# A two-layer block on one core: exponentials divided by their sums inside the rounds, on GpSimd, and the heads' projection as a product of high and low parts

## What is computed

```python
xn = _layernorm(x, axis=-1)
att = jnp.einsum('bhcq,bhCq->bhcC', q, k) / d_query
att = jnp.where(causal, att, -jnp.inf)
p = jax.nn.softmax(att, axis=-1)
y = jnp.einsum('bhcC,bhCv->bhcv', p, v)
z = jnp.einsum('dvh,bhcv->bcd', W, y) * (math.sqrt(d_embed / d_value) / num_heads)
```

## Time and profile before

| | us |
|---|---|
| median of 3 runs | 1225.01 (1225.0 to 1225.53) |
| the profiled execution, its own time | 1223.34 |
| its span | 1221.5 |
| PE busy | 1194.4 (98%) |
| DVE busy | 987.6 (81%) |
| ACT busy | 821.7 (67%) |
| GpSimd busy | 409.0 (33%) |

### The profile page before, as it was taken

One profiled execution on the slowest core, in us unless ns is written; L12 is line 12 of the kernel. 1 busy time (PEld: TensorE's weight loads), 2 busy tenths in 40 slices (PEclk: granted clock), 3 DMA queues, 4 the chain that ended last, 5 costly groups with the idle time before them and its releaser, 6 DMA issues.

```text
span 1221.5 us, 23916 instructions
## 1 busy us (share of the span) xinstructions
PE 1194.4 (98%) x8892; PEld 887.0 (73%) x8892; DVE 987.6 (81%) x1916; ACT 821.7 (67%) x2174; POOL 409.0 (33%) x362
## 2 busy tenths in 40 slices
PE   8999999999999999999999999999999999999997
PEld 6777777767776777677767776777677767767765
DVE  5878588878896889688968896889688878888786
ACT  6775577567755775577567756775577668767775
POOL 2216420640064007300630073007300759326910
PEclk9999999999999999999999999999999999999999
DMA  7014300410041003100410041004100500000000
GB/s 255 1 28 129 101 1 15 137 61 2 20 131 61 1 29 134 50 1 30 134 49 1 30 139 44 2 30 145 38 2 29 159 24 2 10 11 18 1 10 27
DMA packets 44276, 63.93 MB, mean 52 GB/s; under 512 B 8128, under 2 KB 18368, under 8 KB 43904
## 3 DMA queue, kind: packets, MB, share of 16 engines
q1 hardware_dynamic: 44160, 62.39, 16.1%
HBM read 59.48 MB, written 2.88 MB: 51 GB/s over the span
## 4 chain that ended last, share of the span: by engine, by line
PE 85%; DVE 6%; ACT 4%; POOL 2%; issue 1%; DMA 1%; SPq 1%; POOLq 0%; DVEq 0%
PE psum L1445 14%; PE psum L1401 14%; PE psum L1467 12%; PE psum L64 11%; PE psum L66 10%; PE psum L65 10%; PE psum L1504 5%; PE psum L1410 2%; ACT probs L737 2%; PE psum L1353 1%; DVE mneg L1103 1%; PE psum L1471 1%; DVE stats L1212 1%; PE psum L1680 1%; ACT pt L758 1%
## 5 line engine op out<-in xcount | busy, mean ns | idle before, releaser
L737 ACT ACTIVATE probs<-psum,mneg 128x512 f32<-128x512 f32 (+3 forms) x640 | 329.8, 529 | 131.1 <-DVE mneg L1103 126.8
L1103 DVE TENSOR_REDUCE mneg<-psum 128x2 f32<-128x1024 f32 (+2 forms) x320 | 254.4, 821 | 118.4 <-PE psum L1410 118.2
L1445 PE MATMUL psum<-ident,probs 128*128 128x128 f32 x1600 | 224.8, 278 | 9.0 <-ACT pt L758 3.9
L1094 DVE COPY pt<-psum 128x512 f32<-128x512 f32 x320 | 206.1, 683 | 31.4 <-PE psum L1445 29.2
L1445 PEld LDWEIGHTS psum<-ident,probs 128*128 128x128 f32 x1600 | 176.3, 140 | 42.8 <-issue 24.4
L544 POOL TENSOR_TENSOR qk_lo<-sg,qk_hi 128x512 fp32r<-128x512 f32 x64 | 93.3, 1463 | 164.4 <-ACT qk_hi L781 164.4
L508 POOL TENSOR_TENSOR rstd<-var,mhalf 128x4 f32<-128x4 f32 x7 | 7.1, 1011 | 406.0 <-DVE var L990 406.0
L1467 PE MATMUL psum<-pt,v_all 128*64 128x384 f32 (+5 forms) x1088 | 142.6, 412 | 0.0
L737 ACT ACTIVATION_READ_ACCUMULATOR probs<-psum,mneg 128x1 f32 x640 | 132.2, 207 | 0.0
L1401 PE MATMUL psum<-qk_hi 64*128 64x512 f32 (+7 forms) x640 | 121.5, 375 | 1.3 <-ACT probs L737 1.1
L1467 PEld LDWEIGHTS psum<-pt,v_all 128*64 128x64 f32 (+1 forms) x1088 | 69.5, 135 | 66.2 <-issue 50.7
(11 more groups left out here) (261 smaller groups left out, 2415.6 us busy)
## 6 DMA issues: line engine op xcount, KB each, us to landing
crow<-weights SPq DMA_DIRECT2D x256, 128.0 KB, 3.0
rrow<-sums SPq DMA_DIRECT2D x128, 128.0 KB, 3.0
gu_raw<-in_gu SPq DMA_DIRECT2D x1, 2176.0 KB, 12.7
x_all<-in_x SPq DMA_DIRECT2D x8, 256.0 KB, 5.5
out_rows<-x_all SPq DMA_DIRECT2D x8, 256.0 KB, 2.3
down_raw<-in_down SPq DMA_DIRECT2D x1, 1088.0 KB, 14.5
wqkv_raw<-in_wqkv SPq DMA_DIRECT2D x1, 896.0 KB, 8.0
wqkv_raw<-in_wqkv SPq DMA_DIRECT2D x1, 512.0 KB, 6.3
```

What stands on the lines that cost most here:

```text
L737: last = act.activation(probs[:, h * HALF + PROB[t]:h * HALF + PROB[t] + w], bank[score_bank(rnd, c) + h][:, o:o + w], ACT.Exp, bias=mneg[ ...
L1094: dve.tensor_copy(turned_rows(rnd)[:, s % 2, :, 3 - s // 2, :], bank[TURN_BANK[s]].rearrange("p (j q) -> p j q", q=P)).then_inc(pt_ready, 1)
L1103: last = dve.tensor_reduce(mneg_h[:, :, t], psum[:, b:b + 2, o:o + P * (t + 1)], AX, ALU.max, negate=True)
L1445: last = nc.tensor.transpose(bank[TURN_BANK[s]][:, i * P:(i + 1) * P], probs[:, v:v + P], ident[:, :])
```

## The change

Five things are done, and a few small orders go with them.

1. In the first layer each round's exponentials are divided in place. Behind each chunk's exponentials DVE makes the reciprocals of that chunk (`invert_sums0`), and GpSimd multiplies the exponentials by them, one instruction for each head and tile (`norm`); PE's transposes of the first layer wait for that (`normed`) where they waited for `exp_done`. `turn_sums0`, `take_sums0`, the store, the loads and `divide_pair` are gone.
2. `project_out` is made by `split_matmul`: ACT makes the high part of `w_out0` and of each pair's values (`high_values`, after the units of `Y_HIGH_AFTER`), GpSimd the low part (`low_values`, where `divide_pair` stood).
3. The setting up of weights on GpSimd and ACT is spread over the rounds of batch 0; `down` is split in four pieces where it was in two.
4. In `first_head` the score of chunk 1 stands ahead of the third `project_out`. PE waits for `logits_taken` and no longer for `rl_ready`, which is two DVE instructions later. At the start ACT makes the high part of the router's weights behind that of x.
5. At the change of layers DVE no longer waits for `acc_done` ahead of the rows of batch 3. The very last batch's values, division, output rows and store go in two halves of 256 rows, and ACT loads no table for Gelu there.

```diff
+            def norm(n, c):
+
+                pool.wait_ge(rinv0_ready, max_count(n, c) if not first_round(n) else n * NCH + [1, 3, 2][c])
+                for h in ((1, 0) if c == 1 else (0, 1)):
+                    for t in CHUNKS[c]:
+                        v = probs[:, h * HALF + PROB[t]:h * HALF + PROB[t] + P * (t + 1)]
+                        last = pool.tensor_scalar(v, v, rinv0[:, n % 2, h * TILES + t:h * TILES + t + 1], None, ALU.mult)
+                    if c < 2 or h:
+                        last.then_inc(normed, 1)
+
+            def norm_rounds(b, beside):
+                for p in range(PAIRS):
+                    n = b * PAIRS + p
+                    for c in (0, 2, 1):
+                        norm(n, c)
+                    beside(p)
+
+            def low_values(b, p):
+                pool.wait_ge(y_hi_ready, b * PAIRS + p + 1)
+                pool.tensor_tensor(y_lo[:, p, :], yt[:, p, :], y_hi[:, PAIRS - 1 - p, :].bitcast(F32), ALU.subtract).then_inc(y_lo_ready, 1)
...
+            def high_values(b, pairs):
+                for p in pairs:
+                    act.wait_ge(y_ready, b * PAIRS + p + 1)
+                    act.activation(y_hi[:, PAIRS - 1 - p, :], yt[:, p, :], ACT.Copy).then_inc(y_hi_ready, 1)
...
+                    if b == 0 and p >= PAIRS - len(DOWN_PIECES):
+
+                        u = DOWN_PIECES[p - PAIRS + len(DOWN_PIECES)]
+                        act.wait_ge(w_loaded, W_LOADS)
+                        act.activation(down_hi[:, u, :], down_raw[:, u, :], ACT.Copy).then_inc(down_hi_ready, 1)
...
+                        act.wait_ge(act_setup, 1)
+                        act.activation(w_out_hi[:, :, :], w_out0[:, :, :], ACT.Copy).then_inc(w_out_hi_ready, 1)
...
+            def invert_sums0(n, c):
+
+                dve.wait_ge(exp_done, exp_count(n, c))
...
+                dve.reciprocal(dst, src).then_inc(rinv0_ready, 1)
...
                         take_turned(n - 1, range(0, 2))
+                        if p > 1:
+                            invert_sums0(n - 1, 1)
                         row_maxima(n, 0)
-                        invert_sums(n - 1)
                         if p < PAIRS - 1:
                             rest_q(n + 1, SCALE0)
                         elif b:
                             add_rows(b - 1)
                         take_turned(n - 1, [3, 2])
+                        invert_sums0(n, 0)
                         row_maxima(n, 2)
                         if p < PAIRS - 1:
                             rest_k(n + 1)
                         row_maxima(n, 1)
+                        invert_sums0(n, 2)
...
-                pe.wait_ge(exp_done, exp_count(rnd, [0, 0, 1, 1, 2][s]))
+                if rnd < ROUNDS0:
+                    pe.wait_ge(normed, norm_count(rnd, s))
+                else:
+                    pe.wait_ge(exp_done, exp_count(rnd, [0, 0, 1, 1, 2][s]))
...
-                pe.wait_ge(y_divided, b * PAIRS + 2 * i + 2)
+                pe.wait_ge(y_lo_ready, b * PAIRS + 2 * i + 2)
                 for p in (2 * i, 2 * i + 1):
-                    last = mm(ACC, w_out0[:, p, :], yt[:, p, :], start=False, stop=(p == PAIRS - 1), **K)
+                    last = split_matmul(nc, ACC, (w_out_hi[:, p, :], w_out_lo[:, p, :]), (y_hi[:, PAIRS - 1 - p, :], y_lo[:, p, :]), False, p == PAIRS - 1, **K)
...
+                score0(b * PAIRS, 1)
                 if b:
                     project_out(b - 1, 2)
-                score0(b * PAIRS, 1)
...
-            dve.wait_ge(acc_done, B)
+
             norm_rows1(0, G - 1)
...
-                output_rows(G - 1)
+                output_rows(G - 1) if q + 1 < GROUPS else last_rows(G - 1)
```

More of the change, by code:

```diff
@@ L249, in rows1_bank, with last_banks @@
             return bank[3] if g == G - 1 else bank[7]
+        def last_banks(half):
+            return (bank[0], bank[2]) if half else (bank[6], bank[3])
         def copied1(n):
@@ L307, in build @@
         rrow_ready = sem("rrow_ready")
[L308 to L311, removed]
+        rinv0_ready = sem("rinv0_ready")
+        normed = sem("normed")
         y_divided = sem("y_divided")
+        w_out_hi_ready = sem("w_out_hi_ready")
+        w_out_lo_ready = sem("w_out_lo_ready")
+        y_hi_ready = sem("y_hi_ready")
+        y_lo_ready = sem("y_lo_ready")
         y_done = sem("y_done")
@@ L490, in _ @@
                     sp.wait_ge(lin_ready, 1)
-            for b in range(B):
+            for b in range(B - 1):
                 sp.wait_ge(rows_ready, b + 1)
                 sp.dma_start(out_v[b, :, :, :], x_all[:, b, :, :]).then_inc(stored, 16)
-            sp.wait_ge(stored, 16 * B)
+            for half in range(2):
+                t = slice(half * TILES // 2, (half + 1) * TILES // 2)
+                sp.wait_ge(rows_ready, B + half)
+                sp.dma_start(out_v[B - 1, :, t, :], x_all[:, B - 1, t, :]).then_inc(stored, 16)
+            sp.wait_ge(stored, 16 * (B + 1))
         @block.gpsimd
@@ L1452, in turn_sums1 @@
                 transpose_rows(SUMS, spread).then_inc(sums_turned, 1)
-            def turn_sums0(b):
-                pe.wait_ge(rinv_ready, (b + 1) * PAIRS)
-                pe.wait_ge(pt_ready, (b + 1) * PAIRS * (TURNS - 1))
-                nc.tensor.transpose(SUMS[0:PAIRS * 2 * TILES, 0:P], rinv0[:, :], ident[:, :]).then_inc(rinv0_turned, 1)
             def weigh_values(Y, rnd, heads, m):
@@ L1627, in units @@
                 weigh_pair(n)
-                turn_sums0(b)
                 for u in range(2, UNITS):
@@ L1805, in output_rows, with last_rows @@
                     last.then_inc(rows_done, 1)
+                def last_rows(g):
+                    for half in range(2):
+                        pe.wait_ge(y_divided, n0 + g + 1 + half)
+                        for t in range(2 * half, 2 * half + 2):
+                            c = slice(t * P, (t + 1) * P)
+                            last = mm(last_banks(half)[1][:, c], y1t[g][:, c], wo1[:, :], start=True, stop=True)
+                        last.then_inc(rows_done, 1)
                 def head_rows1(r):
```

175 lines of the change are left out of this document (96 added, 79 removed).

## The result

The change made the kernel slower: 1416.51 us median (1414.37 to 1416.88) against 1225.01, a ratio of 1.156 with a 95% interval of 1.1546 to 1.1574. I had forecast 1241 and a range up to 1266. The profiled execution has a span of 1414.3, 192.8 more than before.

The account below looks back on a forecast made before the run. PE was taken to bound the kernel, with 85% of the chain that ended last. Losses of 32.4 less gains of 16.4 made it 16.0 us slower, 1241 for the median of 1225.01; range 1221 to 1266.

Parts of the forecast that it names:

- the four of chunk 1 thus take 1.48: Rounds: GpSimd's four multiplications dividing chunk 1 take 0.47 + 0.25 + 0.47 + 0.29 = 1.48 us.
- upper bound of 2.49: Chunk 1's four GpSimd divisions: at most 2.49 us, if the scalar costs like a second tensor (622 ns for 256 columns).
- my own formulas: Losses from late chunk 1 tiles: ordinary slots 0.22, behind long router steps 0.36, p = 7 1.07, units 1.34; 3.79 a batch.
- The handing over: Around chunk 1's division: 0.30 us from exponentials' end to GpSimd, 0.23 from GpSimd to PE's first matmul.
- PE's waits for GpSimd: Sign ahead of PE's transposes: some 0.2 us in ordinary slots, above 1 in p = 7 and units, 25 to 30 in all.
- dearer scalar: Rival, GpSimd's divisions: each instruction pays its fixed part of 0.18 twice, 0.72 for the four, 1278 us; chance 0.23.
- figure for read commands: GpSimd's divisions: 102 cycles a non-overlapping read command, estimated 0.085 us an instruction, 0.34 for the four, 1258 in all.
- My last sentence: Sign of being wrong: PE waits for chunk 0's or 2's division, so GpSimd is held by something unseen; no size.
- Slot p = 1 costs nothing: Slot p = 1: no loss, since the first round's chunk 1 isn't behind a copy and is made long before.
- The projection's 12.3: Heads' projection: six products of the new kind replace four instructions, gaining 1.54 us a batch, 12.3 in all.
- my 1.5: Last batch, units 7 to 9: ACT's added copies exceed PE's time, costing 1.5 us, between nothing and 4.8.
- Small orders: Gains: turn_sums0 0.9 us, router's logits 0.5, change of layers 1.5, the end 1.2; together 4.1.

Follow-up runs that it names:

- e8: Not the kernel: GpSimd alone, one and two operations by constants or columns, other engines idle; 512 columns took 1.49 us times a constant, 0.62 with plus 0.0.
- e9: Kernel after the change, with plus 0.0 added to each of GpSimd's multiplications by reciprocals: 1268.12 us.
- e10: Kernel after the change, with e9's plus 0.0 and the second layer's weights in six pieces behind GpSimd's divisions in batch 1: 1256.59 us.
- e1: Kernel after the change, GpSimd multiplying the exponentials by the constant 1.0 instead of the reciprocals, so nothing is divided: 1385.55 us.
- e5: Kernel after the change, with eight unread PE transposes between the two stretches of chunk 1's transposes: 1394.41 us.
- e6: Kernel after the change, with the second layer's weights made in six pieces behind GpSimd's divisions in batch 1: 1404.61 us.
- e12: e10's kernel with the heads' projection again in full float32, one product a pair: 1258.86 us.
- e11: Kernel before the change with only the small orders of the change: 1219.98 us against 1225.30 measured beside it.

## Why the prediction was wrong, step by step

**The step that failed** is "the four of chunk 1 thus take 1.48". They take 3.63, above even the upper bound of 2.49, which stood for a scalar that costs like a second tensor. The inference was that all one-input forms of GpSimd lie on one line, since 614 for a copy of 512 and 832 for 768 columns with constants did. e8 shows that this was luck: the 832 belonged to times-and-plus, one of the short pairs. Times alone isn't on the line, with a column or a constant. My bounds came from rows of other operations, so they bounded nothing. Why times alone is slow stays open. In e9, where the four take 1.87, the time is 1268, and in e10, without the batch 0 stall, 1257.

**The structure around it held.** With 3.63 for 1.48 my own formulas give 2.37 for an ordinary slot, 2.51 behind a long router step, 3.22 for p = 7 and 3.49 for the units; the copies give 2.27, 2.27, 3.03 and 3.37. That is 17.8 a batch for my 18.8. The handing over was 0.31 and 0.06, for 0.30 and 0.23. PE's waits for GpSimd showed where I had said, but they are 137 in all and not 25 to 30.

**The rival "dearer scalar"** named the right instruction, for the wrong reason and at the wrong size. It put the price on the scalar, and a constant is nearly as dear (e1: 1.17 for 1.25 on 384 columns); it stopped at fixed parts paid twice, 1278, where the slope is three times mine. The Trainium skill's figure for read commands (page "GPSIMD Engine Reference", section "Performance pitfalls for Q7 kernels") gave 0.34 for the four; the trace shows 2.15 over my sum, and most of it grows with columns, so that isn't what made the change slow. What a column costs over a constant, 0.08 an instruction in e1 and 0.07 in e8 (0.690 for 0.617), is near the 0.085 that I estimated from it; no run shows whether it is the same thing.

**The granted clock** wasn't in the sum at all. With PE's waits under a long GpSimd term it fell to 0.50 in two slots of most batches. That is 25.3 by the slots, 22 by e5. It vanished from the rounds of batches 1 to 7 when work filled a wait (e5, all but two slots) and when the waits shrank (e9).

**GpSimd's queue in batch 0** was missed: 12 by e6, 11.5 by e10. I listed what stands between GpSimd's rounds but took the second layer's weights to be as harmless as before. My last sentence named the mark ("GpSimd is held by something that I don't see here") without looking for it.

**Slot p = 1 costs nothing** was wrong in size: in the kernel after, PE waits 2.4 there, and with e9's form the units of a batch are 1.4 shorter than before in place of 1.2 longer.

**The projection's 12.3** is 2.3 net (e12; 1.2 by the profiled spans). The calls save 1.28 a batch for my 1.54, and 0.76 of it is left at the next copy of values; against that stand 2.4 in the last batch, for my 1.5, and 0.9 in batch 0.

**Small orders** of 3.2 without turn_sums0 were 5.3 (e11); the change of layers gave 1.2 for 1.5 and the end 1.5 for 1.2.

**Batch 0 up to its last copy** is 23.2 longer. Most of that is the same loop: e9's one word leaves 3.4 of it. What GpSimd's splitting, ACT's and the lower clock have in the rest stays open.

## What to carry to other kernels

Price an engine's instruction from rows with the same operations, not from rows with the same shape; where there are none, a bench of twenty instructions settles in one run what bounds from other rows can't. When work moves onto the loop that sets the pace, list everything that its new engine does in program order, once for the whole program: a harmless stretch of 14 us becomes a stall when something starts to wait behind it. And where PE begins to wait, look at its granted clock, and allow for work that runs at half of it.

## What the hardware showed that I had not expected

GpSimd multiplies 512 float32 columns by a scalar in 1.49 to 1.57, by the same scalar spread out as a second tensor in 1.00, and by the scalar plus 0.0 in 0.69. Times-and-minus takes 1.92 where times-and-plus takes 0.62. Beside DVE's products of two SBUF tensors the column form goes from 1.55 to 2.28; beside DVE's copies from PSUM and ACT's copies it doesn't move. And PE's granted clock fell to 0.50 for some 3.5 us behind two waits of 1.08 and 1.15, in four slots behind 0.68 and 1.15, and stayed at 1.00 behind 1.79 and 1.15 at the end of a batch's rounds.
